# Rotated keys turned in 32x32 blocks on VectorE and moved between partitions by DMA

## What is computed

```python
k = _rope(k)                       # rotate: features x tokens
...
def step(kv, inp):                 # chunk by chunk along the tokens
    scores = einsum('bhid,bhjd->bhij', qi, ki) * diag
    o_intra = einsum('bhij,bhje->bhie', scores, vi)
    o_inter = einsum('bhid,bhde->bhie', qi * q_dec, kv)
    kv = blk * kv + einsum('bhjd,bhje->bhde', ki * k_dec, vi)
```

## Time and profile before

| | |
|---|---|
| median of 3 runs | 905.67 us |
| profiled execution, its own time | 905.21 us |
| its span, first to last instruction | 903.4 us |
| PE busy | 895.4 us (99%), 4122 matmuls |
| DVE, ACT, POOL busy | 632.6, 418.6, 373.4 us |
| granted PE clock, mean | 0.999 |
| DMA | 138.55 MB |

### The profile page before, as it was taken

How to read it: one execution, slowest core, us unless ns; L and a number is a source line. 1 busy time by engine, 2 the same in 40 slices (tenths; PEclk the granted TensorE clock), 3 DMA queues, 4 the chain that set the end, 5 groups by cost and what they waited for, 6 DMA issues and landing times.

```text
span 903.4 us, 12444 instructions
## 1 busy us (share of the span) xinstructions
PE 895.4 (99%) x4122; PEld 739.6 (82%) x4122; DVE 632.6 (70%) x905; ACT 418.6 (46%) x705; POOL 373.4 (41%) x276
## 2 busy tenths in 40 slices
PE   8999999999999999999999999999999999999997
PEld 5878888888888888888888888888888888888886
DVE  7978653677653257766777867677767677788797
ACT  3443533443433456444455444463554554634542
POOL 1011112122122475536555456365454563553547
PEclk9999999999999999999999999999999999999999
DMA  6792304379760624413333513244243043264482
GB/s 213 212 398 89 105 24 152 143 254 322 276 223 6 210 94 161 153 43 144 140 117 141 190 55 140 69 181 169 81 163 131 32 178 145 95 234 147 165 259 82
DMA packets 51115, 138.55 MB, mean 153 GB/s; under 512 B 4224, under 2 KB 25344, under 8 KB 45696
## 3 DMA queue, kind: packets, MB, share of 16 engines
q1 hardware_dynamic: 51072, 138.00, 43.2%
HBM read 96.04 MB, written 41.94 MB: 153 GB/s over the span
## 4 chain that ended last, share of the span: by engine, by line
PE 86%; issue 6%; POOL 4%; DVE 3%; ACT 1%; DMA 0%; POOLq 0%; SPq 0%; DVEq 0%; ACTq 0%
PE bank L1274 85%; POOL d_r L1210 2%; POOL rot L1219 1%; PE bank L1332 1%; PE bank L1294 0%; DMA stage<-in_x_nat 0%; DVE tail_sb L1116 0%; PE bank L1448 0%; DVE wst L834 0%; DVE d_sb L1019 0%; DVE tail_sb L1118 0%; ACT mag L522 0%; DVE tail_sb L1102 0%; DVE fz L851 0%; DVE acc L1112 0%
## 5 line engine op out<-in xcount | busy, mean ns | idle before, releaser
L1274 PE MATMUL bank<-xn,aw 128*128 128x512 f32 x960 | 229.1, 390 | 0.0
L1219 POOL TENSOR_TENSOR rot<-rot 128x512 f32<-128x512 f32 x80 | 126.9, 1586 | 234.9 <-DVE rot L1006 234.9
L1274 PEld LDWEIGHTS bank<-xn,aw 128*128 128x128 f32 x960 | 179.0, 188 | 37.3 <-issue 0.7
L1274 PE MATMUL bank<-o_r,ow 128*128 128x512 f32 (+1 forms) x792 | 186.2, 385 | 0.0
L1210 POOL TENSOR_TENSOR d_r<-d_sb,d_r 128x512 fp32r<-128x512 f32 x127 | 166.9, 1339 | 37.2 <-ACT d_r L692 37.1
L1274 PE MATMUL bank<-xn,gu_w 128*128 128x512 f32 x768 | 180.0, 389 | 0.4 <-DVE fz L851 0.4
L1274 PEld LDWEIGHTS bank<-xn,gu_w 128*128 128x128 f32 x768 | 144.1, 188 | 30.9 <-DVE dn_w L843 0.8
L1274 PEld LDWEIGHTS bank<-o_r,ow 128*128 128x128 f32 x792 | 144.4, 188 | 28.5
L1005 DVE TENSOR_TENSOR rot<-bank,rope 128x512 f32<-128x512 f32 x80 | 55.2, 690 | 102.6 <-ACT rot L672 102.5
L671 ACT COPY rot<-bank 64x512 f32<-64x512 f32 x80 | 46.8, 585 | 154.6 <-PE bank L1274 154.2
L692 ACT CAST d_r<-d_sb 128x512 fp32r<-128x512 f32 x128 | 79.0, 621 | 84.6 <-DVE d_sb L1065 62.2
(11 more groups left out here) (87 smaller groups left out, 973.4 us busy)
## 6 DMA issues: line engine op xcount, KB each, us to landing
xn<-xn_split SPq DMA_DIRECT2D x15, 2048.0 KB, 7.8
v_decayed<-vd_split SPq DMA_DIRECT2D x32, 512.0 KB, 3.5
vd_r<-v_decayed SPq DMA_DIRECT2D x16, 1024.0 KB, 7.2
v_r<-v_split SPq DMA_DIRECT2D x16, 512.0 KB, 5.8
wst<-in_mlp_w SPq DMA_DIRECT2D x10, 768.0 KB, 5.2
xn_split<-xn SPq DMA_DIRECT2D x3, 2048.0 KB, 10.7
stage<-in_attn_w SPq DMA_DIRECT2D x4, 1280.0 KB, 5.7
stage<-in_x_nat SPq DMA_DIRECT2D x16, 256.0 KB, 5.0
```

Source lines behind the costliest of these rows:

```text
L1219: pool.tensor_tensor(rot1[:, r % RRING, :], rot1[:, r % RRING, :], rot2[:, r % RRING, :], ALU.add).then_inc(qk_sum, 1)
L1274: last = pe.matmul(dst, a, b, start=start and x == 0, stop=stop and x == len(pairs) - 1)
```

## The change

Nothing of the keys is turned on PE any more, and nothing of them passes through PSUM a second time. DVE turns the split keys `k_r` (high and low part, first 256 tokens) in blocks of 32x32, one instruction for each part, into `kt_sb`; sixteen DMAs move each quarter of 32 partitions by 32 features to its place in `kn_r`. `kn_r` now holds tokens on partitions, and for each feature four words side by side: part (2) by block (2). So the stationary operand of `state` is read with a step of four words. `state` waits for the sixteen transfers.

```diff
-        kn_r = sb("kn_r", [P, 2, VD, DH], F32R)
+        kn_r = sb("kn_r", [P, NQ, Q4, 2, VD], F32R)      # NQ = 4, Q4 = 32
+        kt_sb = sb("kt_sb", [P, NQ, Q4, 2, VD])
...
+            def move_k(n):                                # SP
+                sp.wait_ge(kt_d, 2 * n + 2)
+                for q in range(NQ):
+                    for c in range(NQ):
+                        sp.dma_start(kn_r[c * Q4:(c + 1) * Q4, q].bitcast(F32),
+                                     kt_sb[q * Q4:(q + 1) * Q4, c]).then_inc(kn_in, 16)
...
                         load_v((b + 1) % NB, g + (b + 1) // NB)
+                        move_k(n + 1)
                     if final and b < NB - 1:
                         store_fin(b, 0)
                     if not (final and b >= NB - 2):
                         load_xn(n + 1, (b + 2) % NB)
...
+            move_k(0)
             load_xn(0, 1)
...
-            def kn_round(n):                              # ACT, and its call at r == 2
-                act.wait_ge(kt_d, n + 1)
-                act.copy(kn_r[:, 0, :, :], kt_ps[:, 0:HALF]...).then_inc(kn_hi, 1)
...
-                    if r == RRING:
-                        dve.wait_ge(kt_d, n + 1)
-                    else:
+                    if r > RRING:
                         dve.wait_ge(q_decayed, n * HG + r - RRING)
...
-            def kn_rest(n):                               # DVE, at r == 2
-                dve.wait_ge(kn_hi, n + 1)
-                dve.tensor_tensor(kn_r[:, 1, :, :], kt_ps..., kn_r[:, 0, :, :]..., ALU.subtract)
+            def turn_k(n):                                # DVE, at r == 2
+                dve.wait_ge(qk_lo, n * QK + 1)
+                if_later(n, lambda: dve.wait_ge(kn_in, n * 16 * NQ * NQ))
+                for a in range(2):
+                    dve.transpose(kt_sb[:, :, :, a].rearrange("p c l j -> p j c l"),
+                                  k_r[:, a, 0:HALF]...rearrange("p (j c l) -> p j c l", j=VD, c=NQ)).then_inc(kt_d, 1)
...
-            def transpose_k(n):                           # PE, and its calls after tile 2
...
             def state(n):
-                pe.wait_ge(kn_lo, n + 1)
-                if_later(n, lambda: pe.wait_ge(o_lo, n * NOT))
+                pe.wait_ge(kn_in, n * 16 * NQ * NQ + 16 * NQ * NQ)
+                if is_first(n):
+                    pe.wait_ge(v_lo, NV)
+                else:
+                    pe.wait_ge(o_lo, n * NOT)
                 pe.wait_ge(vd_in, n * 16 + 16)
                 for j in range(VD):
-                    last = products(st_bank(n)[:], [(kn_r[:, a, j, :], vd_r[:, j, c, :]) for a, c in SPLIT],
+                    last = products(st_bank(n)[:], [(kn_r[:, :, :, a, j].rearrange("p q l -> p (q l)"), vd_r[:, j, c, :]) for a, c in SPLIT],
```

More of the change, by code:

```diff
@@ L62 @@
 QK = 1 + HG
+Q4 = 32
+NQ = P // Q4
 VT_AT = {(2, m): 2 * TT + m for m in range(TT)} | {(3, m): 3 * TT + m for m in range(TT)}
@@ L196, in proj_bank @@
             return ([bank[4], bank[5], bank[6], bank[4], bank[5]] if is_first(n) else proj_ps)[tile]
-        kt_ps = bank[7]
         def v_bank(v):
@@ L246, in attention_mlp_kernel @@
         v_in = sem("v_in"); vd_in = sem("vd_in"); state_d = sem("state_d")
-        kt_d = sem("kt_d"); kn_hi = sem("kn_hi"); kn_lo = sem("kn_lo")
+        kt_d = sem("kt_d"); kn_in = sem("kn_in")
         score_d = sem("score_d"); decayed = sem("decayed"); q_decayed = sem("q_decayed")
@@ L672, in turn @@
                 act.copy(rot2[ROT:, r % RRING, :], ps[0:ROT, :]).then_inc(turned, 1)
-            def kn_round(n):
-                act.wait_ge(kt_d, n + 1)
-                act.copy(kn_r[:, 0, :, :], kt_ps[:, 0:HALF].rearrange("p (t e) -> p t e", t=VD)).then_inc(kn_hi, 1)
             def st_round(n):
@@ L704, in projections @@
                         other()
-                    if r == 2:
-                        kn_round(n)
                 for other in beside.get(QK, ()):
@@ L1020, in q_decay_head @@
                                   q_decay[:, h, :], ALU.mult).then_inc(q_decayed, 1)
-            def kn_rest(n):
-                dve.wait_ge(kn_hi, n + 1)
-                dve.tensor_tensor(kn_r[:, 1, :, :], kt_ps[:, 0:HALF].rearrange("p (t e) -> p t e", t=VD),
-                                  kn_r[:, 0, :, :].bitcast(F32), ALU.subtract).then_inc(kn_lo, 1)
+            def turn_k(n):
[3 more added lines that the diff above has]
+                    dve.transpose(kt_sb[:, :, :, a].rearrange("p c l j -> p j c l"),
+                                  k_r[:, a, 0:HALF].bitcast(F32).rearrange("p (j c l) -> p j c l", j=VD, c=NQ)).then_inc(kt_d, 1)
             def st_rest(n):
@@ L1043, in projections @@
                     if r == 2:
-                        kn_rest(n)
+                        turn_k(n)
                     if r == 2 and tables is not None:
@@ L1438, in project, with state @@
                                             for a, c in SPLIT for k in range(KT)]).then_inc(proj_d, 1)
-            def transpose_k(n):
-                pe.wait_ge(qk_sum, n * QK + 1)
-                if not is_first(n):
-                    pe.wait_ge(o_lo, (n - 1) * NOT + 3)
-                else:
[L1446 to L1451, removed]
-                pe.wait_ge(kn_lo, n + 1)
-                if_later(n, lambda: pe.wait_ge(o_lo, n * NOT))
+            def state(n):
+                pe.wait_ge(kn_in, n * 16 * NQ * NQ + 16 * NQ * NQ)
+                if is_first(n):
+                    pe.wait_ge(v_lo, NV)
+                else:
+                    pe.wait_ge(o_lo, n * NOT)
                 pe.wait_ge(vd_in, n * 16 + 16)
                 for j in range(VD):
-                    last = products(st_bank(n)[:], [(kn_r[:, a, j, :], vd_r[:, j, c, :]) for a, c in SPLIT],
+                    last = products(st_bank(n)[:], [(kn_r[:, :, :, a, j].rearrange("p q l -> p (q l)"), vd_r[:, j, c, :]) for a, c in SPLIT],
                                     start=(j == 0), stop=(j == VD - 1))
@@ L1480, in projections @@
                     project(n, tile, g_edge)
-                    if tile == 2:
-                        transpose_k(n)
                     for other in beside.get(tile, ()):
@@ L1582, in _ @@
             project(0, 2, 0)
-            transpose_k(0)
             down(first + 3)
```

## The result

| | before | after |
|---|---|---|
| median | 905.63 us (905.46 to 906.38) | 939.0 us (937.5 to 940.9) |
| ratio to before | | 1.0367 [1.0356, 1.0377] |
| span of the profiled execution | 903.4 us | 935.7 us |
| PE busy | 895.4 us (99%), 4122 matmuls | 901.7 us (96%), 4090 matmuls |

A forecast was written before the change was run, and what follows sets the result against it. PE, busy 99%, was taken to bound the kernel. Span 903.4 less 4.3 for the transposes plus 3.0 for last-group lateness gave 902.1, 903.9 for the execution, and 0.46 more for the median: 904.4 us, range 901.3 to 914.

The forecast's parts named there:

- the second rival: Turned keys reach `state` late in every step, beyond 10.84 us after the turn starts: 917, or 905 to 908; chance 0.23.
- Transposes worth 0.27 a step: On PE, removing two transposes in each of 16 steps gains 0.27 us a step, 4.3 us in all.
- Turns of 0.42 each: On DVE, each of two block turns takes 0.42 us, 0.84 for both; bounds 0.33 and 0.8 each.
- Issues 0.46 apart, bounds 0.375 to 0.70: On SP, sixteen transfer issues start 0.46 us apart, so the last starts 6.9 us after the first.
- Landing 1.9: The last key transfer lands 1.9 us after its issue; bounds 1.5 to 2.8.
- Deadline: In middle steps PE wants the first `state` weights 10.84 us after `turn_k` starts; path 9.7, 1.1 left.
- Last group 3.0 us late: Keys late by 2.1 us in step 14 and 0.5 in step 15, plus 0.4 for DVE in step 13.
- DVE without slack in the last group, 0.4 in step 13: DVE's 0.5 us more work and PE's 0.27 less make the scores of step 14's queries 0.4 late, counted in step 13.
- `load_xn` wanted ten us later, nothing: In the last group `load_xn`, queued behind the sixteen issues, goes out near 838 rather than 834.37, at no cost.
- Strided loads 0: Reading `kn_r` weights in `state` with a step of 16 bytes costs 0, at most 3.0 us.
- Work taken from PE is gained in full: PE, busy 99% of the span, sets the time: work taken from it is gained in full, work added elsewhere is free.
- slower: The sign that the changed kernel measures above 907.5 us; chance given as 0.30.

The follow-up runs named there:

- experiment 6: Changed kernel with the four diagonal key blocks copied by ACT, so SP issues twelve transfers rather than sixteen: 910.0 us, ratio 1.0046.
- experiment 3: Changed kernel with turns and transfers running, but `state` reads unturned `k_r` with the same step and doesn't wait for the transfers: 908.3 us, ratio 1.0027.
- experiment 9: Changed kernel with twelve transfers, turn one projection earlier, and in the last group two of four pairs of final loads behind the transfers and `load_xn`: 905.1 us.
- experiment 7: Changed kernel with the turn one projection earlier and, in the last group, one or two pairs of final loads issued behind the transfers: 908.3 us, ratio 1.0034.
- experiment 2: Kernel before, transposes kept and no transfers, only `kn_r` laid out so that its weights are read with a step of four words: 908.8 us, ratio 1.0034.
- the control: Changed kernel without turns and transfers, `state` reading unturned `k_r` with a step of 16 bytes: 904.0 us, ratio 0.9983.
- experiment 4: Changed kernel with the transfers of three of four steps in each group given other row counts or sent to DRAM: 925.6 us, a single run.

## Why the prediction was wrong

Forecast 904.4 in 901.3 to 914, measured 939.0. The sign was the second rival's, and its rule held: beyond 10.84 us after the start of the turn every 0.1 costs about 1.6 over the kernel. It had reckoned with 11.6, and 12.41 came.

- **Transposes worth 0.27 a step**: right; ordinary steps without them are 0.23 shorter in the mean, with 0.04 lost to the slower loads.
- **Turns of 0.42 each**: 0.62 long, 1.10 for both, 0.26 over my 0.84 and inside the bounds. From the 311 ns of the Trainium skill (VectorE: DVE Perf Modes, "The three transpose paths") for a bf16 block turn of 128 columns I had made an estimate of 0.44; for 256 columns of four-byte elements, written with a step of 16 bytes, the trace shows 0.62. By itself this would have used a quarter of the slack of 1.1 us. `q_decay_head` behind the turns did wait less, as forecast: 0.58 us long rather than 1.18.
- **Issues 0.46 apart, bounds 0.375 to 0.70: the step that failed.** 0.632, 15 x 0.17 = 2.5 us more, more than twice the slack. The value lay within my bounds, but the second rival took 0.47 for it. My bound of 0.70 would have given 10.5 us for the issues and a price near what came; I had it in the text and no case for it. What I had no row for was a transfer with both ends in SBUF, and I took rows with one end in DRAM for it because they matched in another respect.
- **Landing 1.9**: right, 1.86 in the middle and 1.80 to 1.90 in the last group of the changed kernel. Only in experiment 6 it was longer, 3.4 and 3.1 in steps 14 and 15; my upper end of 2.8 was too low for that.
- **Deadline**: right to the hundredth. 1.57 late by the sum, 1.36 + 0.23 lost.
- **Last group 3.0 us late**: 9.9 us of waits, and 3.2 for the clock that I had not thought of. Step 13 was taken to be in time and idled 2.58. For step 14 I had SP free 1.9 us after the turn and a short row of issues behind that; it was free 0.3 after it, and the row took 10.2. It is the same failed step again. The 9.5 us that I allowed from the turn to the weights of step 14 were right (9.4).
- **DVE without slack in the last group, 0.4 in step 13**: not seen in the changed kernel, where no wait of PE for DVE's scores stands beside the wait for the keys. It shows once the keys are in time: weight loads wait 1.2 us for DVE's low parts in experiment 3, and the 0.46 of experiment 9 is of this kind.
- **`load_xn` wanted ten us later, nothing**: wrong in the last group once the keys' own wait is gone; 1.4 us in experiments 3 and 7.
- **Strided loads 0**: 0.04 a step, with 0.31 us a load. The Trainium skill's rule (Advanced Engine Details and Errata, "SBUF Cachelines"), that an access to another line each time pays, agrees with the durations: 310 ns rather than 188. But the loads are hidden as I had reckoned. What I had not reckoned with is the 2.3 us that the new layout costs at the edges by itself (experiment 2).
- **Work taken from PE is gained in full**: not at the edges. Which of POOL and DVE comes first there turned round, and that took 2.3 us back in the control. An earlier PE is not the shown cause, since experiment 2 has the same with the transposes in place. The trace of before had both rows; I had not read it for operations that are 0.05 us apart.
- **Sums**: a few were off without changing anything. With a third of rival 2 within 3 us of the forecast, 0.15 of it is slower and not 0.19, so slower had 0.26; all 4.6 gained would be 901.1 and not 901.3; the upper ends for steps 14 and 15 are 3.2 and 1.6 us late, not 3.3 and 1.8.

Left open and not tried: a run that tests whether the last microsecond between experiment 9 and the control is DVE's extra work; the removal of the transposes with dense loads; and the issues on another queue than SP's.

## What to carry to other kernels

Before a chain of small transfers is put on a deadline, count issues x interval and take the interval from transfers with the same kinds of ends; here it was three quarters of the path. Where a bound multiplies by fifteen, the bound and not the likely value decides whether there is a rival, and it needs a chance of its own. Where all middle steps are in time, what is left sits in the last group, where outputs queue on the same engine and the same DMAs: put what the bound engine waits for first.

## What was new of the hardware

- Back to back on SP, a transfer inside SBUF is issued 0.632 us after the one ahead with 1, 16 or 32 rows, and 0.643 with 128; from SBUF to DRAM it is 0.464, with 512 or 128 bytes a row (experiment 4).
- A weight load with a step of 16 bytes lasts 0.31 us rather than 0.19 and still nearly hides under matmuls of 512 columns (0.04 us more for six); a copy or subtraction of 256 columns that writes so takes 1.5 to 1.7 times as long (0.62 rather than 0.37 or 0.42).
- After some long pauses the granted clock falls to 1.2 GHz, and about eight of PE's matmuls start 0.427 us apart rather than 0.227. The pauses of 3.37 (experiment 4), 3.40, 3.59, 3.61, 3.75 and 4.24 us did this, and so did one of 2.49 (experiment 6); those of 2.16, 2.58, 3.00, 3.19 and 3.30 (experiment 4) did not. What decides is open; the length of the pause alone doesn't.
